# A state-space scan on VectorE: two 512-column scans joined into one of 1025 columns, decays in SBUF instead of PSUM

## The reference, cut to what matters

```python
dA = jnp.exp(dt_t[..., None] * A)                                # decay
h = dA * h + dt_t[..., None] * B_t[:, None, :] * x_t[..., None]  # state
y = jnp.sum(h * C_t[:, None, :], axis=-1)                        # sum over the 16 states
```

## Time and profile before

| | |
|---|---|
| median of 3 timed runs | 1363.04 us |
| lowest, highest | 1359.74, 1366.42 us |
| profiled execution, first to last instruction (span) | 1358.3 us |
| profiled execution's own total time | not listed; the lowest timed run is 1.44 us above the span |
| busy over the span | PE 1079.5 (79%), DVE 881.0 (65%), ACT 685.8 (50%), POOL 559.6 us (41%) |
| scan stage | from the first scan's start at 58.7 to the last one's end at 286.5 us |

### The profile page before, as it was taken

The page is one execution under the profiler, slowest core; times in us unless marked ns, Lnnn a source line. Parts: engine busy times, 40 slices in busy tenths (PEclk is TensorE's granted clock), DMA queues, the critical chain, the costliest instruction groups (busy, mean ns, idle before and its releaser), DMA issues. The chain is left out here.

```text
span 1358.3 us, 25046 instructions
## 1 busy us (share of the span) xinstructions
PE 1079.5 (79%) x8292; PEld 708.4 (52%) x8292; DVE 881.0 (65%) x2989; ACT 685.8 (50%) x1268; POOL 559.6 (41%) x740
## 2 busy tenths in 40 slices
PE   8877777778189553299936999969977999899998
PEld 3222232336188553299934777744434777654544
DVE  6799999976455456377549888843648878840201
ACT  4786656644044301133206888737856888541221
POOL 4489988853633314544426444100025555100000
PEclk9799999998599765599978999989997999999999
DMA  2997000002422206211120000020612000000000
GB/s 63 206 202 126 0 1 0 1 0 71 140 61 57 92 7 219 70 41 44 37 74 1 2 3 3 2 53 6 203 47 89 3 2 3 2 1 0 16 0 16
DMA packets 85742, 66.77 MB, mean 49 GB/s; under 512 B 15102, under 2 KB 70412, under 8 KB 85612
## 3 DMA queue, kind: packets, MB, share of 16 engines
q1 hardware_dynamic: 79916, 53.65, 17.3%
q0 software_dynamic: 4544, 9.38, 1.9%
q10 hardware_dynamic: 1152, 2.10, 0.4%
HBM read 36.52 MB, written 28.59 MB: 48 GB/s over the span
## 5 line engine op out<-in xcount | busy, mean ns | idle before, releaser
L1076 POOL TENSOR_TENSOR hC<-h,Cs 128x1024 f32<-128x1024 f32 x64 | 150.8, 2356 | 35.3 <-DVE h L973 34.7
L786 PE MATMUL bank<-hC,ident 128*128 128x512 f32 x256 | 128.1, 624 | 45.1 <-POOL hC L1076 43.0
L973 DVE TENSOR_TENSOR_SCAN h<-bank,state,dBx 128x512 f32<-128x512 f32 x128 | 157.3, 1271 | 2.2
L1457 POOL DMA_INDIRECT moe_answers<-moe_yw,moe_xg x78 | 83.7, 1073 | 128.9 <-DVE moe_yw L1634 70.9
L2608 DVE CUSTOM_DVE_ANT_0 decay_below<-bank,decay_q_mask 128x256 bf16<-128x256 f32 x256 | 97.3, 419 | 23.3 <-PE bank L2420 22.4
L786 PEld LDWEIGHTS bank<-hC,ident 128*128 128x128 f32 x256 | 44.9, 192 | 103.9 <-POOL hC L1076 67.1
L2608 DVE CUSTOM_DVE_ANT_0 window_below<-bank,window_q_mask 128x192 bf16<-128x192 f32 x256 | 80.3, 353 | 28.6 <-PE bank L2420 27.0
L2548 ACT ACTIVATE decay_pb<-bank 128x512 f32<-128x512 f32 x128 | 76.2, 598 | 33.5 <-PE bank L2435 32.6
L885 ACT ACTIVATE bank<-dt,A 128x512 f32<-128x512 f32 x128 | 83.2, 683 | 18.7 <-DVE h L973 17.4
L1528 PE MATMUL bank<-moe_xgT,moe_wac 128*128 128x128 f32 x624 | 86.4, 284 | 6.5 <-issue 4.0
L1543 PE MATMUL bank<-moe_wd,moe_hT 128*128 x624 | 83.2, 278 | 5.7 <-DVE moe_hT L1621 2.5
(11 more groups left out here) (482 smaller groups left out, 2797.2 us busy)
## 6 DMA issues: line engine op xcount, KB each, us to landing
moe_slots<-blank SPq DMA_DIRECT2D x16, 1040.0 KB, 16.9
deep_rows<-token_weights SPq DMA_DIRECT2D x32, 256.0 KB, 3.9
moe_xg<-moe_slots SPq DMA_DIRECT2D x78, 65.0 KB, 1.9
moe_wa<-in_moe_w SPq DMA_DIRECT2D x2, 2048.0 KB, 9.7
moe_back<-moe_answers SPq DMA_DIRECT2D x8, 256.0 KB, 5.3
moe_back<-moe_answers ACTq DMA_DIRECT2D x8, 256.0 KB, 6.0
moe_wu<-in_moe_wu SPq DMA_DIRECT2D x1, 2048.0 KB, 15.4
deep_w<-in_deep_w SPq DMA_DIRECT2D x3, 512.0 KB, 6.5
```

The costliest lines, as they stand in the source:

```text
L786: last = nc.tensor.matmul(sum_bank(hh)[:], k.ident[:], hC[:, u % 2, hh, :], start=(n == 0), stop=(n == NS - 1))
L973: v.tensor_tensor_scan(h[:, u % 2, hh, :], decay_bank(u, hh)[:], dBx[:, u % 2, hh, :], state[:, n, hh:hh + 1], ALU.mult, ALU.add).then_inc ...
L1076: g.tensor_tensor(hC[:, u % 2], h[:, u % 2], Cs[:, u % 2, None, :].to_broadcast([P, H, CW]), ALU.mult).then_inc(q_hC, 1)
L1457: nc.gpsimd.indirect_dma_start(answers, bass.IndirectOffsetOnAxis(index, 0), yw[:, i % NY, :], None)\
```

## The change

The two scans of a step become one instruction over 2*512+1 columns. `h`, `dBx` and the decays get rows of 513 columns per half. Column 512 of the first half is a resetting column: its decay is 0 (written once, `cut`) and its `dBx` is the start value of the second half (written each step by ACT, `second_state`), so that the running value becomes that start value there. The decays lie in SBUF, over `xpad`. The scan now waits for both decays and for `second_state`. PE no longer waits for all scans ahead of the feed-forward part's first product, since banks 0 to 3 are free.

```diff
--- before.py
+++ after.py
@@ -314,7 +314,7 @@
         w2b = sb("m_w2b", [P, P])
 
         xo = sb("xo", [P, T, P])
-        xpad = sb("xpad", [P, PAD + N])
+        xpad = sb("xpad", [P, max(PAD + N, 2 * H * (CW + 1))])
         both = sb("both_norms", [P, T])
         sz = sb("sz", [P, H, N])
         xc = sb("xc", [P, H, N])
@@ -325,14 +325,14 @@
         chosen = sb("chosen", [P, BC])
         rt1, rt2 = sb("rt1", [P, 2, CW]), sb("rt2", [P, 2, CW])
         lr = sb("lr", [R, 2, CW])
-        dBx = sb("dBx", [P, 2, H, CW])
-        h = sb("h", [P, 2, H, CW])
+        dBx = sb("dBx", [P, 2, H, CW + 1])
+        h = sb("h", [P, 2, H, CW + 1])
         hC = sb("hC", [P, 2, H, CW])
         Cs = sb("Cs", [P, 2, CW])
         diag = taps_w[:, 0, :].rearrange("p (h q) -> p h q", h=H)
         Bs = taps_w[:, 1, :].rearrange("p (b w) -> p b w", b=2)
         xi = k.xnT
-        conv = dBx[:, :, 0, :]
+        conv = dBx[:, :, 0, 0:CW]
         yT = sb("yT", [P, H, CW])
         state = sb("state", [P, NS, H])
 
@@ -357,6 +357,7 @@
         names = ("b", "c", "dA", "cs", "dBx", "h", "hC", "st", "y", "yc")
         q_b, q_c, q_dA, q_cs, q_dBx, q_h, q_hC, q_st, q_y, q_yc = (k.sem("q_" + n) for n in names)
         q_bs, q_rest, q_diag = k.sem("q_b_copied"), k.sem("q_dBx_rest"), k.sem("q_diag")
+        q_cut, q_first = k.sem("q_cut"), k.sem("q_first")
         shared = lambda u: max(0, u - FIRST_SHARED)
         o_mm, o_x1 = k.sem("o_mm"), k.sem("o_x1")
         d_dt, d_dtx = k.sem("d_dt"), k.sem("d_dtx")
@@ -367,7 +368,8 @@
         U = C * NS
         hT = [dtx[:].rearrange("p h n -> p (h n)")[:, b * FB * CW:(b + 1) * FB * CW].rearrange("p (f w) -> p f w", f=FB)
               for b in range(2)]
-        decay_bank = lambda u, hh: bank[2 * (u % 2) + hh]
+        decay = xpad[:, 0:2 * H * (CW + 1)].rearrange("p (b h w) -> p b h w", b=2, h=H)
+        joined = lambda a, u: a[:, u % 2].rearrange("p h w -> p (h w)")[:, 0:2 * CW + 1]
         sum_bank = lambda hh: bank[4 + hh]
         b_bank, c_bank = bank[6], bank[7]
 
@@ -814,7 +816,7 @@
             def hidden(c):
                 pe.wait_ge(f_tev, c + 1)
                 if c == 0:
-                    pe.wait_ge(q_h, H * U)
+                    pe.wait_ge(s_raw, H * C)
                 for f in range(FB):
                     if (c, f) == (3, 3):
                         r.ranks(pe, 0)
@@ -868,22 +870,32 @@
 
         def scan_scalar(act, take_rates, take_high):
             def keep_state(u):
-                act.wait_ge(q_h, H * (u + 1))
+                act.wait_ge(q_h, u + 1)
                 nc.scalar.activation(state[:, u % NS, :], h[:, u % 2, :, CW - 1], ACT.Copy).then_inc(q_st, 1)
+
+            def cut():
+                act.wait_ge(c_zero, 1)
+                nc.scalar.activation(decay[:, :, 0, CW], k.mhalf[:, 0:2], ACT.Copy, scale=0.0).then_inc(q_cut, 1)
+
+            def second_state(u):
+                wait(act, q_st, u - NS + 1)
+                nc.scalar.activation(dBx[:, u % 2, 0, CW:CW + 1], state[:, u % NS, 1:2], ACT.Copy).then_inc(q_first, 1)
 
             for u in range(U):
                 c, n = divmod(u, NS)
                 if u == 0:
                     act.wait_ge(s_A, 2)
                     act.wait_ge(s_dt, 1)
-                if u == 1:
-                    act.wait_ge(s_raw, H * C)
                 if n == 0:
                     wait(act, d_dt, H * c)
-                wait(act, q_h, H * (u - 1))
+                wait(act, q_h, u - 1)
                 for hh in range(H):
-                    nc.scalar.activation(decay_bank(u, hh)[:], dt[:, hh, cols(c)], ACT.Exp,
+                    nc.scalar.activation(decay[:, u % 2, hh, 0:CW], dt[:, hh, cols(c)], ACT.Exp,
                                          scale=A[:, hh, n:n + 1]).then_inc(q_dA, 1)
+                if u == 0:
+                    cut()
+                    act.wait_ge(c_more, 1)
+                second_state(u)
                 if u == 0:
                     take_rates(last_c - 1)
                     take_high(last_c)
@@ -968,10 +980,12 @@
                 wait(dve, q_rest, shared(u + 1))
                 wait(dve, q_hC, u - 1)
                 wait(dve, q_st, max(u - 1, (u - NS + 1) if c else 0))
-                for hh in range(H):
-                    dve.wait_ge(q_dA, H * u + hh + 1)
-                    v.tensor_tensor_scan(h[:, u % 2, hh, :], decay_bank(u, hh)[:], dBx[:, u % 2, hh, :],
-                                         state[:, n, hh:hh + 1], ALU.mult, ALU.add).then_inc(q_h, 1)
+                if u == 0:
+                    dve.wait_ge(q_cut, 1)
+                dve.wait_ge(q_dA, H * (u + 1))
+                dve.wait_ge(q_first, u + 1)
+                v.tensor_tensor_scan(joined(h, u), joined(decay, u), joined(dBx, u), state[:, n, 0:1], ALU.mult, ALU.add)\
+                    .then_inc(q_h, 1)
                 if u == 0:
                     first_rest(last_c)
                 if c and n == 3:
@@ -1070,10 +1084,10 @@
                                 Bs[:, u % 2, None, :].to_broadcast([P, H, CW - WD]), ALU.mult).then_inc(q_rest, 1)
 
             for u in range(U):
-                pool.wait_ge(q_h, H * (u + 1))
+                pool.wait_ge(q_h, u + 1)
                 pool.wait_ge(q_cs, u + 1)
                 wait(pool, q_y, u - 1)
-                g.tensor_tensor(hC[:, u % 2], h[:, u % 2], Cs[:, u % 2, None, :].to_broadcast([P, H, CW]),
+                g.tensor_tensor(hC[:, u % 2], h[:, u % 2, :, 0:CW], Cs[:, u % 2, None, :].to_broadcast([P, H, CW]),
                                 ALU.mult).then_inc(q_hC, 1)
                 c, n = 1 + (u - 5) // 4, (u - 5) % 4
                 if 1 <= c < C:
```

## The result

The changed kernel takes 1446.9 us (median of 4, 1445.22 to 1450.19) against 1362.28 us: a ratio of 1.0615, 95% interval 1.0584 to 1.0645. That is 84.6 us slower; forecast were +95 and 1458 us, range 1443 to 1492. The profiled run took 1448.3 us with a span of 1446.6.

What follows compares the result with a forecast made beforehand. DVE's own instructions were taken to bound the stage; after the change, scan and POOL turns would make its 63 periods 321 us against 225.4, +95 on the 1363.0 us median: 1458 us, range 1443 to 1492.

Steps and rivals of the forecast that it cites:

- Taking turns: Scan stage: the scan with two SBUF inputs and POOL's SBUF-reading products exclude each other; 95.7 us added.
- Rival A: Scan stage: the scan does not take turns with POOL; -5.9 us, about 1357 us; chance 0.09.
- D: Joined scan: the change has no effect on the time; 1363 us; chance 0.02.
- B: Scan stage: scan and POOL interleave in part, each slowed but not stopped; +45, about 1408 us; chance 0.04.
- Scan's stream 2.15: DVE's joined scan: its 1025 columns stream for 2.15 us (2.11 to 2.29) in each step.
- Blocked L1069 0.54: POOL's share of `dBx` in 43 steps: waiting behind the scan, it adds 0.54 us a step.
- Blocked 512-column piece 1.08: POOL's softplus piece (L1050 or L1054) in 12 steps: waiting behind the scan, it adds 1.08 us a step.
- the ring: Scan stage: scan and `hC` wait for each other in turn, 4.57 us a bare step, up to 5.6 with other POOL work.
- `hC` 2.356: POOL's product of `h` and `Cs`: 2.356 us in each step, 2.31 where it follows another POOL operation.
- 312, the low end: Scan stage: with 0.31 us hidden behind each of 55 blocked operations and the cheaper column, 312 us, +86.
- C, dearer handoffs: Scan stage: POOL and scan cost full durations; +125 to +130, about 1490 us; chance 0.12 beyond 1480.
- the upper sum: Scan stage: every POOL and scan duration counted in full, 351 us, +125.

Runs made afterwards that it cites:

- e1: Kernel before with only the decays moved to SBUF, still two scans of 512 columns a step: 1462.24 us, ratio 1.0749.
- e2: Kernel before with only the two scans joined into one of 1024 columns, decays still in PSUM, reset left out: 1358.75 us, ratio 0.9985.
- e5: Changed kernel with two idle columns between the buffers of `h`, so the second starts at column 1028, not 1026: 1463.23 us, ratio 1.0692.
- e4: Kernel before with `h`, `hC` and `Cs` at other column offsets in each pair of steps, to read `hC` durations: 1360.58 us (one run).

## Why the prediction was right, and where it was off

- **Taking turns.** Right, and shown by e1 against e2: the two-input scan in SBUF alone costs more than the whole change does, joining alone costs nothing. That a scan behaves as L555 in the earlier trace rows was an inference from another operation; the handoffs of 2.15, 1.08, 0.53 and 0.51 us confirm it. Rival A (1357 us) is out by 90 us, D (1363) by 84, B (1408) by 39: neither engine got between the other's reads.
- **The terms of the step.** Scan's stream 2.15: measured 2.15 and 2.16. Blocked L1069 0.54: 0.51. Blocked 512-column piece 1.08: the timeline has 3.25 us for L1068 and L1064, where the ring's 2.15 and 1.08 give 3.23. The instruction alone 2.345: 2.35. `second_state` 194 ns: 187. Decays on ACT 717: 715.
- **The term that was off** is `hC`, "`hC` 2.356" in all steps: it was 1.99 in 32 of them. 32 x 0.36 = 11.5 us of the sum's 321, and the measured stage was 310.1. e5 starts both buffers at slow places and gets 320.5. The prediction put the 513-column rows at nothing and gave no reason; no column was added for POOL, but the rows changed where its operands start against each other.
- **What was luck.** The measured 310.1 us lie below 312, the low end that was worked out, and +84.6 below its +86. The range holds 1446.9 because it was drawn "a little below" that bound, not because a term allowed for it.
- **A term that the sum left out** came to almost nothing. Before, about 10 of the 225.4 us are DVE's work once per chunk (L946, L951) and single waits, in steps of up to 5.54 us. In the changed kernel the turns cover them: beyond the pattern stand the first step (5.23 us) and one more (5.68).
- **The price of place.** L555 and L3218 said that SBUF or PSUM makes no difference to DVE's own time. It holds: 2.352 us for 1025 columns from SBUF alone, 2.349 for 1024 from PSUM in e2. The Trainium skill's shorter fixed cost for an SBUF source ("VectorE: DVE Perf Modes", the TRN2 errata) did not show here either.
- **Joining.** 0.115 us a step was put into rival A; e2 has 0.05 to 0.06, in all steps. In the changed kernel the scan's fixed part counts for little in any case: a blocked scan hides it.
- **C, dearer handoffs, and the upper sum.** Out: a waiting instruction hides its fixed part in every handoff that was read, and steps from step 21 on were 4.97 and 4.63 us, not 5.4. The sum of full durations, 351 us, is 41 too long.
- **ACT and PE.** Right: ACT's own wait for a scan rose to 74.9 us, so it has slack, and `second_state` held up a scan once, for 0.4 us, at step 1. PE's granted clock over the stage went from 0.97 to 0.87; some of the sums run at the lower level (3.46 us for four products from 205.17 on, where the granted clock was 0.57, against 1.98 from 200.19 on at 1.00), and the steps around them are still 4.97 and 4.63 us.

## What to carry to other kernels

Before an operand of a DVE instruction is moved from PSUM to SBUF, count the SBUF tiles that it then reads: with two, it took turns here with every large POOL product that reads SBUF, and where the one needs the other's result, as `hC` needs `h`, the step costs the sum of both streams, not the larger. One place in the trace where such a pair already meets prices it. When a tile is padded by an odd number of columns, ask against which other operand it now starts, and read each buffer's instruction for itself and not the mean of the group.

## What was not expected of the hardware

POOL's two-input product of 1024 fp32 columns takes 2.35 us or 2.00 us, by the difference of the two inputs' starts within 16 bytes: 0 or 4 bytes slow, 8 or 12 bytes fast, 2.18 with one half of each (e4). Two shifted tiles and a wider share turn that into 0.7% of the whole kernel.

A busy row of an instruction that waits for its turn to read looks the same as work: 3.8 us for a 2.35 us scan, 2.55 us for a 0.73 us product, and DVE 99% busy in a stage that it did not bound.
